# First layer norm, query product and the first steps of an attention merged into one block, by groups of four batches

## The reference

```python
def _layernorm(x, axis=-1, eps=1e-05):
    m = jnp.mean(x, axis=axis, keepdims=True)
    v = jnp.var(x, axis=axis, keepdims=True)
    return (x - m) / jnp.sqrt(v + eps)
...
# x: (16, 112, 256), ctx_1024: (16, 375, 256); first attention, 16 heads of 16
q = jnp.einsum('btd,hdk->bhtk', tgt, Wq) + bq[None, :, None, :]
k = jnp.einsum('bsd,hdk->bhsk', src, Wk) + bk[None, :, None, :]
v = jnp.einsum('bsd,hdk->bhsk', src, Wv) + bv[None, :, None, :]
scores = jnp.einsum('bhtk,bhsk->bhts', q, k) * scale
weights = jax.nn.softmax(scores, axis=-1)
out = jnp.einsum('bhts,bhsk->bhtk', weights, v)
...
x = x + jnp.tanh(g_xattn[0]) * _L0_xattn_ref(_layernorm(x, axis=-1), ctx_1024, ...)
x = x + jnp.tanh(g_ffn[0]) * _L0_ffn_ref(_layernorm(x, axis=-1), ...)
```

## Time and profile before

| | |
|---|---|
| median of 3 runs (lowest to highest) | 1180.03 us (1177.42 to 1182.08) |
| the profiled execution | 1178.83 us |
| its span, mean granted clock of PE | 1176.9 us, 0.888 |
| PE busy | 866.1 us (74%) |
| DVE busy | 660.0 us (56%) |
| ACT busy | 507.0 us (43%) |
| POOL busy | 321.9 us (27%) |
| DMA | 84905 packets, 85.19 MB |

### The profile page before, as it was taken

How to read it: one execution, slowest core, us unless ns; L and a number is a source line. 1 busy time by engine, 2 the same in 40 slices (tenths; PEclk the granted TensorE clock), 3 DMA queues, 4 the chain that set the end, 5 groups by cost and what they waited for, 6 DMA issues and landing times. The chain is left out here.

```text
span 1176.9 us, 23500 instructions
## 1 busy us (share of the span) xinstructions
PE 866.1 (74%) x7667; PEld 681.5 (58%) x7667; DVE 660.0 (56%) x1561; ACT 507.0 (43%) x1064; POOL 321.9 (27%) x327
## 2 busy tenths in 40 slices
PE   2402799999987385469999995578784888989870
PEld 1101476667666385469777774467673666666650
DVE  5610577777775788456333331566763455555548
ACT  2101366555654355312333331345553566666650
POOL 0012333333310135860000002466651222222220
PEclk9755899999999677789999998798896899999995
DMA  2366222222210336530222224396310000000002
GB/s 62 89 161 212 70 72 64 63 64 63 55 35 2 96 89 223 187 119 6 69 67 66 64 64 120 91 228 184 89 53 1 1 0 1 0 1 0 0 1 62
DMA packets 84905, 85.19 MB, mean 72 GB/s; under 512 B 23718, under 2 KB 76118, under 8 KB 84822
## 3 DMA queue, kind: packets, MB, share of 16 engines
q1 hardware_dynamic: 77574, 71.47, 21.6%
q0 software_dynamic: 6144, 11.96, 3.9%
q10 hardware_dynamic: 1104, 0.64, 0.2%
HBM read 52.90 MB, written 16.25 MB: 59 GB/s over the span
## 5 line engine op out<-in xcount | busy, mean ns | idle before, releaser
L615 DVE TENSOR_REDUCE a_mx<-ps 112x2 f32<-112x750 f32 x128 | 119.8, 936 | 42.6 <-PE ps L508 38.5
L1955 POOL TENSOR_TENSOR f_rl<-f_rf,f_rh 128x448 bf16<-128x448 f32 x64 | 66.2, 1035 | 188.2 <-DVE f_rh L1983 188.2
L51 PE MATMUL ps<-f_w2hi,f_hh 128*128 (+1 forms) x292 | 84.0, 288 | 42.6 <-DVE f_hl L1310 42.4
L579 ACT ACTIVATE a_Pf<-ps 125x672 f32<-125x672 f32 x128 | 89.8, 730 | 13.1 <-PE ps L456 12.0
L1308 DVE CAST f_hh<-f_hf 128x512 bf16<-128x512 f32 (+1 forms) x57 | 33.5, 589 | 109.4 <-ACT f_hf L1166 84.4
L1936 ACT ACTIVATE f_rf<-ps,f_ln 128x112 f32<-128x112 f32 x256 | 91.9, 437 | 0.9 <-PE ps L1912 0.9
L1463 POOL DMA_INDIRECT a_yg<-f_yd,pos x32 | 32.8, 1024 | 209.4 <-POOLq L88 201.0
L51 PE MATMUL ps<-f_w2hi,f_rh 128*112 128x256 bf16 x256 | 73.4, 287 | 20.2 <-POOL f_rl L1955 20.2
L51 PE MATMUL ps<-f_w2hi,f_hl 128*128 (+1 forms) x292 | 83.6, 286 | 0.0
L51 PE MATMUL ps<-f_w2lo,f_hh 128*128 (+1 forms) x292 | 83.5, 286 | 0.0
L51 PE MATMUL ps<-f_xgThi,f_w1hi 128*128 128x128 bf16 x328 | 73.7, 227 | 7.7 <-issue 5.1
(11 more groups left out here) (353 smaller groups left out, 2558.5 us busy)
## 6 DMA issues: line engine op xcount, KB each, us to landing
f_raw<-F_w SPq DMA_DIRECT2D x28, 512.0 KB, 4.1
a_ctxF<-ctxT SPq DMA_DIRECT2D x16, 375.0 KB, 3.2
a_cT<-ctxT SPq DMA_DIRECT2D x16, 375.0 KB, 6.6
a_cR<-ctx SPq DMA_DIRECT2D x16, 375.0 KB
a_stkQ<-a_QS SPq DMA_DIRECT2D x48, 112.0 KB, 2.3
f_xd<-a_zero SPq DMA_DIRECT2D x1, 5248.0 KB, 18.2
f_xg<-f_xd SPq DMA_DIRECT2D x41, 128.0 KB, 2.1
f_yd<-f_yo SPq DMA_DIRECT2D x41, 128.0 KB, 1.7
```

What stands on the lines that cost most here:

```text
L51: ins = nc.tensor.matmul(out, l, r, start=first and i == 0, stop=last and i == len(steps) - 1)
L579: nc.scalar.activation(Pf[:, s % PB], psST[:C, s % 2, :SC, :QW], ACT.Exp).then_inc(exp_done, 1)
L615: nc.vector.reduce_max(mx[:, n.odd, 2 * j:2 * j + 2], psMX[:T, :, :S], AX).then_inc(mx_red, 1)
L1955: nc.gpsimd.tensor_tensor(rl[:, t.odd], rf[:, t.odd], rh[:, t.odd], ALU.subtract).then_inc(r_lo, 1)
```

## The change

`setup`, `normalise`, `load_square` and the query block are removed; their work goes into the attention's block, which becomes the first block of the kernel. In detail:

- `x` is loaded in four groups of four batches on SP's queue, with the first two contexts between them; weights, gates and biases are loaded from ACT's queue.
- Moments, roots, norms, transposes and query products run per group, interleaved with keys and values of batch 0. The high parts of the weights and of `QS` are made on ACT, the low parts of the weights on POOL. The scaling of `Wo` and `bo` moves to ACT.
- `QS` has two slots of one group each instead of room for all; a group waits for the transfers of the group two before it. Groups 0 and 2 go to `stkQ` from SP's queue, groups 1 and 3 from POOL's. On POOL the pieces of keys of batch 0 come behind the transfers of group 1, and those of batch 1 behind those of group 3.
- `Pf` takes the memory of the start-up's tiles, so ACT waits for all groups before the first exp, and PE before the maxima of batch 2.
- The zero fill of `xd` is cut into 16 transfers of 328 rows, one at the end of every step with a batch `b`, from a tile of 41 partitions repeated 8 times. SP waits for all of them at the end of the block.

The core of the diff:

```diff
-        setup(nc, k, a["x"], a["g_xattn"], a["g_ffn"])
-        normalise(nc, k, "n0")
...
-        l0_attention(nc, k, a["ctxT"], a["L0_Wq"], a["L0_bq"], a["L0_Wk"], a["L0_bk"], a["L0_Wv"], a["L0_bv"],
-                     a["L0_Wo"], a["L0_bo"], xd)
+        l0_attention(nc, k, a, xd)
...
-        zero = sb("zero", [P, D], F32)
+        FILL = NBLK * P // B
+        FILL_ROWS = 8
+        zero = sb("zero", [FILL // FILL_ROWS, D], F32)
...
+        raw = k.sb("a0_raw", [P, 4, KD, D], F32, early)
+        qf = k.sb("a0_qf", [P, 2, GT], F32, early)
+        QS = k.sb("a0_QS", [P, QN, 2, GB, KD, 2, T], BF16, early)
...
-            emit(None, None, None, None, (ring(0),), (ring(0), ring(1)))
-            emit(None, None, None, ring(0), (ring(1),), (ring(2),))
             emit(None, None, ring(0), ring(1), (ring(2),), (ring(3),))
...
+        def stack_queries(eng, g):
+
+            eng.wait_ge(q_lo, (g + 1) * KD * 2)
+            for jj in range(JJ):
+                for i, part in ((0, 0), (1, 0), (2, 1)):
+                    eng.dma_start(stkQ[32 * i:32 * i + 32, rows(g), :, jj, :],
+                                  QS[32 * jj:32 * jj + 32, g % QN, part].rearrange("p b t h q -> p b t (h q)"))\
+                        .then_inc(q_in[g], 16)
...
-                sp.wait_ge(zero_set, 1)
-                sp.dma_start(xd.rearrange("(n p) d -> p n d", p=P),
-                             zero[:].unsqueeze(1).broadcast_to([P, NBLK, D])).then_inc(k.filled, 16)
...
+                def fill(b):
+                    sp.dma_start(xd[bass.ds(b.b * FILL, FILL), :].rearrange("(p r) d -> p r d", r=FILL_ROWS),
+                                 zero[:].unsqueeze(1).broadcast_to([FILL // FILL_ROWS, FILL_ROWS, D])).then_inc(k.filled, 16)
...
                     if n is not None:
                         place_maxima(n, 0)
+                    if b is not None:
+                        fill(b)
...
+                tokens(0)
+                tokens(1)
+                load(ring(0))
+                tokens(2)
+                tokens(3)
+                load(ring(1))
+                sp.wait_ge(one_set, 1)
+                for r in range(2):
+                    sp.dma_start(stkK[96 + r:97 + r].rearrange("o a t j s -> o (a t j s)"), one[:]).then_inc(ones_in, 16)
+                stack_queries(sp, 0)
+                emit(None, None, None, ring(0), (ring(1),), (ring(2),))
+                stack_queries(sp, 2)
+                sp.wait_ge(zero_set, 1)
                 run(sp, emit)
+                sp.wait_ge(k.filled, 16 * B)
...
+                turn_tokens(0)
+                turn_tokens(1)
+                queries(0, 0)
+                queries(0, 1)
+                pe.wait_ge(w_lo, 2)
+                keys(ring(0), 0)
+                turn_tokens(2)
+                queries(1, 0)
+                queries(1, 1)
+                keys(ring(0), 1)
+                turn_tokens(3)
+                pe.wait_ge(w_lo, 3)
+                vals(ring(0), 0)
+                queries(2, 0)
+                queries(2, 1)
+                vals(ring(0), 1)
+                queries(3, 0)
+                queries(3, 1)
+                pe.wait_ge(q_copied, KD * NG)
                 pe.wait_ge(ones_in, 32)
-                pe.wait_ge(v_ones, 1)
+                pe.wait_ge(q_in[0], 3 * JJ * 16)
...
+                def queries(g):
+                    if g == 0:
+                        act.wait_ge(b_in, 48)
+                        act.wait_ge(pair_done, 1)
+                    for m in range(KD):
+                        n = KD * g + m
+                        act.wait_ge(q_full, n + 1)
+                        at_least(act, q_lo, 2 * (n - 1))
+                        nc.scalar.activation(qf[:, m], queried(n), ACT.Identity, bias=bias[:, 0, m:m + 1]).then_inc(q_copied, 1)
+                        act.wait_ge(q_copied, n + 1)
+                        if g >= QN:
+                            act.wait_ge(q_in[g - QN], 3 * JJ * 16)
+                        for h in range(2):
+                            nc.scalar.activation(QS[:, g % QN, 0, :, m, h, :], qf[:, m].rearrange("p (b q) -> p b q", q=T), ACT.Copy,
+                                                 scale=pair[:, h:h + 1]).then_inc(q_hi, 1)
...
+                high(0)
+                deviation(0)
+                high(1)
+                deviation(1)
+                x_high(0)
+                cast(ring(0))
+                high(2)
+                deviation(2)
+                x_high(1)
+                queries(0)
+                project(ring(0), 0)
+                deviation(3)
+                x_high(2)
+                queries(1)
+                project(ring(0), 1)
+                x_high(3)
+                cast(ring(1))
                 act.wait_ge(v_ones, 1)
+                project(ring(0), 2)
+                queries(2)
+                project(ring(0), 3)
...
+                high(3)
+                act.wait_ge(bo_in, 16)
+                nc.scalar.activation(bo_b[:], bo_b[:], ACT.Copy, scale=k.tg_x[:T, 0:1]).then_inc(bo_scaled, 1)
+                queries(3)
...
+                low(0)
+                low(1)
+                emit(None, None, None, None, (ring(0),), ())
+                low(2)
+                stack_queries(pool, 1)
+                emit(None, None, None, ring(0), (ring(1),), ())
+                low(3)
+                stack_queries(pool, 3)
                 run(pool, emit)
...
+                moments(0)
+                normed(0)
+                moments(1)
+                normed(1)
+                x_low(0)
+                moments(2)
+                normed(2)
+                x_low(1)
+                queries(0)
+                low_keys(ring(0), 0)
+                moments(3)
+                normed(3)
+                x_low(2)
+                queries(1)
+                low_keys(ring(0), 1)
+                x_low(3)
+                queries(2)
+                queries(3)
```

More of the change, by code:

```diff
@@ L273, in l0_attention @@
         sem = lambda name: k.sem("a0_" + name)
-        wq, wk, wv, wo = load_square(nc, k, "a0", [Wq, Wk, Wv, Wo], [None, None, None, k.tg_x[:, 0:1]], ctx)
+        JJ = P // (2 * DH)
+        NJ = KD * JJ
+        QN = 2
+        parts = [[sb(f"w{n}_{p}", [P, KD, D], BF16) for p in ("hi", "lo")] for n in "qkvo"]
+        wq, wk, wv, wo = parts
         bias = sb("bias", [P, 3, KD], F32)
@@ new lines, in cast, with high, deviation @@
+                def cast(row):
+                    act.wait_ge(ctx_in[row.odd], row.half * 16 + 16)
+                    at_least(act, proj_full, row.b * TASKS - 2 * TASKS + TASKS)
+                    nc.scalar.activation(ctxH[:, row.odd], ctxF[:, row.odd], ACT.Copy).then_inc(ctx_hi, 1)
+                def high(i):
+                    act.wait_ge(wl_in[i], 16)
+                    nc.scalar.activation(parts[i][0][:], raw[:, i], ACT.Copy).then_inc(w_hi, 1)
+                def deviation(g):
+                    act.wait_ge(var_done, GB * (g + 1))
+                    act.wait_ge(eps_set, 1)
+                    nc.scalar.activation(root[:, rows(g)], k.mv[:, rows(g), 1], ACT.Sqrt, bias=eps[:, 0:1]).then_inc(root_done, 1)
@@ L608, in _, with moments @@
             def _(dve):
-                nc.vector.memset(one[:], 1.0).then_inc(one_set, 1)
+                def moments(g):
+                    dve.wait_ge(x_in[g], 16)
+                    for b in range(GB * g, GB * (g + 1)):
+                        nc.vector.bn_stats(stats[:, b, :], k.xs[:, b, :]).then_inc(st_done, 1)
+                    for b in range(GB * g, GB * (g + 1)):
+                        dve.wait_ge(st_done, b + 1)
+                        nc.vector.bn_aggr(k.mv[:, b, :], stats[:, b, :]).then_inc(var_done, 1)
@@ new lines, in normed @@
+                def normed(g):
+                    dve.wait_ge(root_done, g + 1)
+                    nc.vector.reciprocal(k.rstd[:, rows(g)], root[:, rows(g)]).then_inc(rstd_done, 1)
+                    dve.wait_ge(rstd_done, g + 1)
+                    for b in range(GB * g, GB * (g + 1)):
+                        nc.vector.tensor_scalar(k.xn[:, b, :], k.xs[:, b, :], k.mv[:, b, 0:1], k.rstd[:, b:b + 1],
+                                                ALU.subtract, ALU.mult).then_inc(xn_done, 1)
```

351 lines of the change are left out of this document (119 added, 232 removed).

## The result

The changed kernel takes 1191.47 us (median of 4 runs, 1189.94 to 1191.98) against 1179.40 for the kernel before on the same chip (4 runs, 1177.42 to 1182.08): a ratio of 1.0099, interval 1.0076 to 1.0122. It is 12 us, or 1.0%, slower. The forecast was 1172, faster by 0.6%; 1191.5 lies in its range, on the other side of no change. The profiled execution took 1191.97 us with a span of 1190.3, 13.4 more than before.

What follows compares the result with a forecast made beforehand. Before T0 latency and order, not engine work, bound the kernel; from the attention's loop on TensorE was busy 14.5 of 15 us. Winning 70 us ahead of T0 and losing 62 behind gave 1170.9, median 1172; range 1152 to 1206.

Steps and rivals of the forecast that it cites:

- POOL as second queue: Start-up: POOL issues the query transfers of groups 1 and 3 at 0.53 us each.
- T0: Start of the second batch's maxima, where the start-up ends: forecast at 64 us, 70 earlier than 134.06.
- the next step is 13.9 to 14.1 us long as before: Start-up: from first maxima at 47.5 us, the first step keeps its old length, so T0 would be 61.4.
- POOL's second round: Start-up: POOL's group 3 queries from 47.1 to 53.5 us, low part, six pieces of keys and landing give T0 60.4.
- The fill goes to one DMA engine: Attention loop: each fill's 328 packets of 46 ns run alone on one engine, 15.1 us.
- most of the gain is given back: Attention loop: the sixteen fills lose 62 of the 70 us won ahead of T0.
- SP's round: Attention loop: SP's issues from one fill to the next, with rows held behind the fill, take 17.8 us a step.
- TensorE's path: Attention loop: scores waiting for minus-maxima rows behind the fill make two steps 36.8 us, 18.4 each.
- The sum: Whole kernel: 1178.8 - 7.9 = 1170.9 us, 1172 on the median.
- POOL pays per run: Rival, start-up: POOL's query transfers cost four times as much, T0 about 100, time 1208 us; chance 0.22.
- The fill dealt over many engines: Rival, attention loop: a fill takes 1.1 us, all 70 us of gain remain, time 1110 us; chance 0.12.
- The loop suffers more than counted: Rival, attention loop: packets of 49 ns or a step of 19, 16 to 18 us more, 1189; chance 0.14.

Runs made afterwards that it cites:

- e9: Changed kernel with each fill's source on 4 partitions spaced 4 apart (0, 4, 8, 12) instead of 41 partitions: 1110.6 us, ratio 0.940 to the kernel before.
- e10: e9 with 40 extra matmuls on TensorE in the start-up, before the first maxima, results overwritten: 1117.6 us, ratio 0.950 to the kernel before.
- e1: Changed kernel with each fill's source laid out as 8 partitions with 41 repeats instead of 41 with 8: 1108.1 us, ratio 0.942 to the kernel before.
- e3: Changed kernel with each fill's source laid out as 4 neighbouring partitions with 82 repeats: 1192.1 us, ratio 1.011 to the kernel before.
- e4: Changed kernel with 40 extra matmuls a step on TensorE before its wait for the second pair of minus-maxima rows: 1195.7 us, ratio 1.014 to the kernel before.
- e13: Changed kernel with the pieces of keys dealt 3 to SP and 9 to POOL instead of 6 and 6: 1184.4 us, ratio 1.003 to the kernel before.
- e14: e13 with 20 extra matmuls a step on TensorE before the wait for the second half's rows: 1168.0 us, ratio 0.990 to the kernel before.
- e12: Changed kernel with each fill issued by POOL behind the pieces of keys instead of by SP: 1194.8 us, ratio 1.013 to the kernel before.

## Why the prediction was wrong, step by step

**POOL as second queue, T0.** Right in its mechanism and in the price of 0.53 (0.584). T0 was 66.75 for 64, and two terms failed. The first is "the next step is 13.9 to 14.1 us long as before": the first maxima came at 47.91 for 47.5, but the first step took 18.8, as TensorE, after 5.3 us of waiting, ran all of it at 1.2 GHz (granted clock 0.50 from 46 to 67 us). I took the slow clock only "until 33 us"; at half clock TensorE's part of the step is 5.1 us longer (e9 against e10). But a full clock alone would not have brought T0 forward: e1 had it back and still waited for the pieces until 66.51. The second is POOL's second round, "60.4". QS 3 was ready at 50.2 for 47.1, the twelve transfers took 0.6 more, and the pieces landed 4.2 to 6.3 us after their issue where I took 2.2: from 50 to 65 us the 16 DMA engines were full in the kernel after (busy share 0.99 to 1.06), and I had added up issues there, not bytes. 60.4 + 3.1 + 0.6 + 2.5 (a landing of 4.7, the median) is 66.6. The 2.6 us that I had added for handovers hid part of it.

**The fill goes to one DMA engine, 328 packets of 46 ns.** Right: 45 ns and one engine in the trace. That most of the gain is given back was right in kind; e1 against the kernel after shows 83 us given back where I had 62.

**SP's round, 17.8 us.** This is the step that failed most. The mechanism was right, the terms were too small, each by a little:

| from fill to fill | forecast | measured (182.22 to 202.35) |
|---|---|---|
| fill's issue to the end of the held rows | 12.0 | 12.45 |
| load | 0.4 | 1.17 |
| six pieces | 4.0 | 3.93 |
| two rows | 1.4 | 1.60 |
| gaps between different lines | 0 | 0.98 |
| sum | 17.8 | 20.13 |

The gaps of 0.2 to 0.3 belong to the eight steps that the program runs as a loop with register addresses. The trace of before has them there (pieces end at 205.56, the next row is issued at 205.79); I had read the step of the earlier trace rows, which is written out, and there the gap is 0.04 (147.27 to 147.31). In a written-out step of the kernel after the round is 19.0 (102.77 to 121.78), and the mean over 13 steps is 19.8. The load's 0.4 holds where no slow fill is still at work (0.40 in e1); behind one it took 1.17 here and 3.3 in e3.

**TensorE's path, 18.4 us.** Wrong by the sentence "TensorE's clock I leave: it stays at full clock". After each wait for the rows the clock was 1.2 GHz for several us (granted 0.50 from 199 to 203 us, after the wait until 198.96). The same stretch, from the late scores to the turn of the next maxima, in the kernel after and in e1:

```profile
198.96 0.80 PE L279 MATMUL ps<-a_stkQ,a_stkK 98*125 x3 [4.40 <-DMA a_stkQ<-a_cneg]
...
207.54 0.26 PE L342 MATMUL ps<-ident,a_mx 112*8 112x112 f32 x1
```

```profile
213.57 0.45 PE L279 MATMUL ps<-a_stkQ,a_stkK 98*125 x3
...
219.53 0.26 PE L342 MATMUL ps<-ident,a_mx 112*8 112x112 f32 x1
```

8.58 us against 5.96: 2.6 more. On a path of two steps that is 1.3 a step, which with 18.4 gives 19.7, beside SP's 19.9. It was hidden behind SP's round (e4) and appears as soon as that is shortened (e13 to e14, 1.5 a step).

**The sum.** 13 steps at 19.77 for 18.1 are 21.7 us, T0 2.7, and the last two steps took 13.9 each for 15.4 (-3.0); what is left of the landing and the first fill is under 0.5. That makes some 21 us on the profiled execution of 1191.97 against 1170.9. With SP's round shortened by the 2 us that I had missed and the clock held at the level I had assumed, e14 takes 1168.0; I had forecast 1172.

**The rivals.** *POOL pays per run* fell with the trace. *The fill dealt over many engines* did not happen. Its 1110 is close to the 1108.1 of e1, but by luck in part: a fill takes 6.7 us there (328 KB at 50 GB/s), not 1.1, and is only hidden. *The loop suffers more than counted*, "packets of 49 ns or a step of 19", at 1189, is what happened, and by the step. Its 0.14 was too low for a case in which three small terms (gaps, the load, the clock) all pointed one way.

## What to carry to other kernels

Before a transfer is cut up, count how many DMA engines its slowest dimension can be dealt to and how many SBUF ports its partitions reach: 41 partitions gave one engine for 15 us, 4 neighbours gave four engines behind one port, and 4 partitions spaced by 4 moved the same bytes in some 3.8 us (82 packets of 46 ns each). In a loop that a queue closes, add up each issue with its gap and at the price it has behind the slow transfer; terms of a few tenths, 1.7 us a step in all, times 13 steps turned a gain into a loss. Where transfers follow each other closely, add up their bytes too: the pieces of keys landed after 4.7 us and not after 2.2 while all DMA engines were busy. And where two paths lie within half a microsecond, an experiment that relieves one of them shows little (e4 none, e13 7 us of 23.5): relieve both before a cause is ruled out.

## What the runs showed of the hardware that was not expected

- Packets of 1 KB from two, four or eight neighbouring partitions, each with an engine of its own, take 81, 148 and 148 ns (26, 25, 50 GB/s); from four partitions 32 apart 79 ns (51 GB/s), 4 apart 46 ns (95 GB/s). On one engine, from 41 partitions, they start 45 ns apart (23 GB/s).
- A DMA engine that is occupied by one queue's transfer holds the other queues' issue: in e12 POOL issues the fills and SP's six pieces of keys take 9.4 us in one step and 3.9 in the next.
- The same fill costs SP 0.71 us to issue and POOL 2.49. POOL's leaves 1328 packets in place of 329, by the counts of its queue (28544 against 7296 packets for 16 fills); SP's 69158 fell to 63894:

```profile
L539 POOL DMA_DIRECT2D f_xd<-a_zero x16: 2472/2491/3079, 80.8 to 353.7; - x16
```
